# First expert matmul of a two-layer attention and mixture-of-experts kernel as three fp32r passes, split on GpSimd

## The reference

```python
# layer 0, in _moe
h = jax.nn.gelu(jnp.einsum('td,edf->etf', xf, w1) + b1[:, None, :], approximate=False)
eo = jnp.einsum('etf,efd->etd', h, w2) + b2[:, None, :]
out = jnp.einsum('etd,te->td', eo, combine)
# layer 1, in moe_ffn: eight experts and one shared one
h = jnp.einsum('nd,ehd->neh', xf, exp_w1)
h = jax.nn.silu(h)
eo = jnp.einsum('neh,edh->ned', h, exp_w2)
```

## Time and profile before

| | |
|---|---|
| time, median of 3 runs | 4743.52 us (4737.04 to 4760.26) |
| the profiled execution's own time | 4747.16 us |
| its span | 4745.7 us |
| PE busy | 4555.6 us (96%) |
| PEld busy | 2804.6 us (59%) |
| DVE busy | 3607.6 us (76%) |
| ACT busy | 2699.7 us (57%) |
| POOL busy | 696.7 us (15%) |
| mean granted clock of TensorE | 0.979 |
| HBM read | 237.40 MB |

### The profile page before, as it was taken

The page is one execution under the profiler, slowest core; times in us unless marked ns, Lnnn a source line. Parts: engine busy times, 40 slices in busy tenths (PEclk is TensorE's granted clock), DMA queues, the critical chain, the costliest instruction groups (busy, mean ns, idle before and its releaser), DMA issues.

```text
span 4745.7 us, 104925 instructions
## 1 busy us (share of the span) xinstructions
PE 4555.6 (96%) x40946; PEld 2804.6 (59%) x41312; DVE 3607.6 (76%) x9823; ACT 2699.7 (57%) x5505; POOL 696.7 (15%) x853
## 2 busy tenths in 40 slices
PE   6999999999999999999999999999999999999999
PEld 3465556666555666655565556655566556655566
DVE  5867776767777777777768888788878888788875
ACT  1566666666666667665565555555455555555554
POOL 2111212111211211121110111011110111101100
PEclk8999998999999999999999999999999999999999
DMA  2222222222222222223233323332233323332222
GB/s 68 39 52 54 50 54 59 67 58 60 48 53 54 61 67 60 58 53 75 66 99 81 80 61 89 87 89 62 76 101 81 85 61 85 103 81 79 62 70 74
DMA packets 168008, 327.22 MB, mean 69 GB/s; under 512 B 25656, under 2 KB 76624, under 8 KB 167520
## 3 DMA queue, kind: packets, MB, share of 16 engines
q1 hardware_dynamic: 167520, 320.49, 27.6%
HBM read 237.40 MB, written 4.19 MB: 51 GB/s over the span
## 4 chain that ended last, share of the span: by engine, by line
PE 79%; DVE 14%; ACT 3%; issue 2%; SPq 0%; DMA 0%; POOL 0%; DVEq 0%
PE sums L961 16%; PE b L1022 10%; PE b L1034 10%; PE b L832 9%; PE b L943 7%; PE b L933 7%; DVE chunk_max L1075 5%; PE b L856 4%; PE b L917 3%; DVE nm_s L1064 3%; DVE b L1081 3%; PE b L884 2%; ACT probs_c L1232 2%; PE b L996 2%; PE b L908 2%
## 5 line engine op out<-in xcount | busy, mean ns | idle before, releaser
L1232 ACT ACTIVATE probs_c<-b 128x512 f32<-128x512 f32 (+1 forms) x3584 | 1738.3, 572 | 1073.0 <-PE b L943 1065.0
L1081 DVE CUSTOM_DVE_ANT_0 b<-b,mcross_q 128x512 f32<-128x512 f32 (+1 forms) x2048 | 1121.1, 605 | 212.0 <-PE b L832 209.7
L1075 DVE TENSOR_REDUCE chunk_max<-b 128x1 f32<-128x512 f32 x1536 | 973.1, 683 | 139.4 <-PE b L832 134.2
L961 PE MATMUL sums<-probs_c,vc 128*32 128x256 f32 x13312 | 930.1, 395 | 0.6 <-ACT o_c L1236 0.3
L832 PE MATMUL b<-kc,qc 32*128 32x512 f32 (+1 forms) x4096 | 822.1, 412 | 17.4 <-DVE chunk_max L1075 7.1
L1034 PE MATMUL b<-w_back,hidden 128*128 128x128 f32 x4352 | 565.4, 281 | 15.5 <-DVE vc L1138 12.0
L1034 PEld LDWEIGHTS b<-w_back,hidden 128*128 128x128 f32 x4352 | 529.6, 194 | 74.6 <-ACT probs_c L1232 24.1
L832 PEld LDWEIGHTS b<-kc,qc 32*128 32x128 f32 x4096 | 425.6, 187 | 249.3 <-ACT probs_c L1232 93.2
L961 PEld LDWEIGHTS sums<-probs_c,vc 128*32 128x32 f32 x13312 | 348.0, 111 | 340.0 <-issue 166.4
L943 PE MATMUL b<-qc,kc 32*128 32x256 f32 (+1 forms) x6656 | 515.0, 336 | 17.3 <-DVE chunk_max L1077 2.2
L1022 PE MATMUL b<-xT_e,w_in 128*128 128x256 f32 x2176 | 528.5, 388 | 0.2 <-DVE chunk_max L1081 0.2
(11 more groups left out here) (159 smaller groups left out, 4497.1 us busy)
## 6 DMA issues: line engine op xcount, KB each, us to landing
w_in<-in_experts SPq DMA_DIRECT2D x272, 256.0 KB, 3.1
w_back<-in_experts SPq DMA_DIRECT2D x272, 256.0 KB, 3.3
kc<-k_hi SPq DMA_DIRECT2D x1024, 50.0 KB
ctxT<-in_ctxT SPq DMA_DIRECT2D x32, 800.5 KB, 5.2
kc<-k_lo SPq DMA_DIRECT2D x512, 50.0 KB
mask_words<-in_mcross SPq DMA_DIRECT2D x32, 800.5 KB
mask_words<-in_mcrossT SPq DMA_DIRECT2D x32, 768.0 KB
out_x<-xe SPq DMA_DIRECT2D x32, 128.0 KB, 2.0
```

What stands on the lines that cost most here:

```text
L961: last = pe.matmul(acc[HP * j:HP * j + HP, :], T["vc"][x.p][0:x.kn, v0:v0 + HP], probs_of(T, x)[0:x.kn, j, half:half + S], start=x.j == 0, ...
L1075: done = dve.tensor_reduce(best[:, x.i:x.i + 1], tile, AX, ALU.max)
L1081: done = dve.tensor_tensor_reduce(part, part, mask, 1.0, -3e38, ALU.add, ALU.max, best[:, qt:qt + 1])
L1232: act.activation(probs_of(T, x)[0:x.kn, x.j, 0:n], tile[0:x.kn, 0:n], ACT.Exp, scale=SCALE).then_inc(M["a_read"], 1)
```

## The change

The first expert product is no longer one fp32 matmul for each block, but three fp32r matmuls into the same bank: high weights by high tokens, high weights by low tokens, low weights by high tokens. (The low-by-low product is left out.) POOL makes the parts with two new steps: `EP`, one for each expert (a rounding `tensor_scalar` of 128 x 512 and a subtraction `tensor_tensor`, into `w_high` and `w_low`, two buffers of each), and `XP`, one for each round (the same for the 128 x 256 tokens). EF waits for both. `w_in` has one buffer instead of two; its next load waits for EP on POOL (`w_split`), not for EF on PE, and is issued right behind that EP in the order. EP waits for the load and for the EF that last used its pair of high and low buffers. The planner's figure for EF goes from 0.87 to 0.66, and it has figures for EP and XP. As the planner merges lists by these figures, the order of every engine is another than before.

```diff
-         "R2": 3.0, "R3": 3.0, "EBT": 1.5, "EBM": 1.0, "NS": 1.5, "ML": 8.0}
+         "R2": 3.0, "R3": 3.0, "EBT": 1.5, "EBM": 1.0, "NS": 1.5, "ML": 8.0, "EP": 2.0}
...
-POOL_US = {"LN2": 3.1, "RM2": 1.5, "RS": 0.75}
+POOL_US = {"LN2": 3.1, "RM2": 1.5, "RS": 0.75, "EP": 1.5, "XP": 0.8}
...
-        "EF": 0.87, "EBT": 0.2, "WV": 0.43, "LX": 3.0, "CL": 8.0, "KD": 10.0, "ML": 8.0, "EL": 4.0, "ST": 3.0}
+        "EF": 0.66, "EBT": 0.2, "WV": 0.43, "LX": 3.0, "CL": 8.0, "KD": 10.0, "ML": 8.0, "EL": 4.0, "ST": 3.0}
...
     def experts(self, l, p):
         count = E0 if l == 0 else E1 + 1
         out = []
+        out += self.load_expert(l, 0, 0)
         for e in range(2):
-            out += self.load_expert(l, e, 0) + self.load_expert(l, e, 1)
+            out += self.load_expert(l, e, 1)
         out += self.output(l, p)
+        out += self.split_expert(l, 0)
...
             out.append(self.put("xeT", "XT", "normed_e", l=l, role="e", p=p))
+        out.append(self.put("x_split", "XP", "xeT", l=l, p=p))
+        out += self.split_expert(l, 1)
         out.append(self.put("rt", "RT", "xeT", l=l, p=p))
...
         if l == 0:
             for e in range(0, count, 2):
+                if e:
+                    out += self.split_expert(l, e) + self.split_expert(l, e + 1)
                 piece = self.hidden(l, p, e)
                 if e:
                     piece += self.expert_out(l, p, e - 1)
                     piece += self.load_expert(l, e + 1, 1)
                 piece += self.hidden(l, p, e + 1)
-                for one in (e, e + 1):
-                    piece += self.load_expert(l, one + 2, 0) if one + 2 < count else []
                 piece += self.expert_out(l, p, e)
                 piece += self.load_expert(l, e + 2, 1) if e + 2 < count else []
                 out.append(piece)
...
         for e in range(count + 1):
             if e < count:
+                if 0 < e < count - 1:
+                    out += self.split_expert(l, e + 1)
                 out.append(self.hidden(l, p, e))
-                out += self.load_expert(l, e + 2, 0) if e + 2 < count else []
...
     def hidden(self, l, p, e):
         out = []
         for half in range(2):
-            step = self.put(("hidden", e), "EF", "xeT", l=l, p=p, i=e, c=half)
-            step.of["load"] = self.at["load", 0, e]
+            step = self.put(("hidden", e), "EF", "x_split", l=l, p=p, i=e, c=half)
+            step.of["split"] = self.at["split", e]
             out.append(step)
-        self.at["free", 0, e % EXPERT_SLOTS] = step
+        self.at["halves_free", e % EXPERT_SLOTS] = step
         return out
+
+    def split_expert(self, l, e):
+        step = self.put(("split", e), "EP", l=l, i=e)
+        step.of["load"] = self.at["load", 0, e]
+        step.of["halves_free"] = self.at.get(("halves_free", e % EXPERT_SLOTS))
+        self.at["free", 0, 0] = step
+        return [step] + (self.load_expert(l, e + 1, 0) if e + 1 < (E0 if l == 0 else E1 + 1) else [])
...
     def load_expert(self, l, e, part):
 
         step = self.put(("load", part, e), "EL", l=l, i=e, j=part)
-        step.of["free"] = self.at.get(("free", part, e % EXPERT_SLOTS))
+        step.of["free"] = self.at.get(("free", part, e % EXPERT_SLOTS if part else 0))
         return [step]
...
         elif x.kind == "EL":
-            x.slot = x.i % EXPERT_SLOTS
+            x.slot = x.i % EXPERT_SLOTS if x.j else 0
             x.c = loaded.get((x.j, x.slot), 0)
             loaded[x.j, x.slot] = x.c + 1
...
         elif x.kind == "EF":
-            load = x.of["load"]
+            slot = x.i % EXPERT_SLOTS
             if x.c == 0:
-                pe.wait_ge(M["expert_loaded", 0, load.slot], 16 * (load.c + 1))
+                pe.wait_ge(M["x_split"], nth(x.of["x_split"]))
+                pe.wait_ge(M["w_split"], nth(x.of["split"]))
             for half in range(2):
-                f = 2 * x.c + half
-                last = pe.matmul(tile[:, half * S:(half + 1) * S], T["w_in"][load.slot][:, f * P:(f + 1) * P],
-                                 T["xT_e"][:], start=True, stop=True)
+                acc, some = tile[:, half * S:(half + 1) * S], slice((2 * x.c + half) * P, (2 * x.c + half + 1) * P)
+                pe.matmul(acc, T["w_high"][slot][:, some], T["x_high"][:], start=True, stop=False)
+                pe.matmul(acc, T["w_high"][slot][:, some], T["x_low"][:], start=False, stop=False)
+                last = pe.matmul(acc, T["w_low"][slot][:, some], T["x_high"][:], start=False, stop=True)
             last.then_inc(M["a_made"], 1)
...
+        elif x.kind == "XP":
+            pool.wait_ge(M["a_read"], in_ring(x.of["xeT"]))
+            pool.tensor_scalar(T["x_high"][:], T["xT_e"][:], 1.0, 1.0, ALU.mult, ALU.mult).then_inc(M["x_rounded"], 1)
+            pool.wait_ge(M["x_rounded"], nth(x))
+            pool.tensor_tensor(T["x_low"][:], T["xT_e"][:], T["x_high"][:].bitcast(F32), ALU.subtract).then_inc(M["x_split"], 1)
+        elif x.kind == "EP":
+            load = x.of["load"]
+            high = T["w_high"][x.i % EXPERT_SLOTS][:]
+            pool.wait_ge(M["expert_loaded", 0, load.slot], 16 * (load.c + 1))
+            if "halves_free" in x.of:
+                pool.wait_ge(M["a_made"], in_ring(x.of["halves_free"]))
+            pool.tensor_scalar(high, T["w_in"][:], 1.0, 1.0, ALU.mult, ALU.mult).then_inc(M["w_rounded"], 1)
+            pool.wait_ge(M["w_rounded"], nth(x))
+            pool.tensor_tensor(T["w_low"][x.i % EXPERT_SLOTS][:], T["w_in"][:], high.bitcast(F32),
+                               ALU.subtract).then_inc(M["w_split"], 1)
...
         elif x.kind == "EL":
-            if "free" in x.of:
-                sp.wait_ge(M["d_made" if x.j else "a_made"], in_ring(x.of["free"]))
-            sp.dma_start(T["w_back" if x.j else "w_in"][x.slot][:],
+            if "free" in x.of and x.j:
+                sp.wait_ge(M["d_made"], in_ring(x.of["free"]))
+            elif "free" in x.of:
+                sp.wait_ge(M["w_split"], nth(x.of["free"]))
+            sp.dma_start(T["w_back"][x.slot][:] if x.j else T["w_in"][:],
                          t["experts"][x.l * E0 + x.i, :, x.j * FF:(x.j + 1) * FF]
                          ).then_inc(M["expert_loaded", x.j, x.slot], 16)
...
-        "hidden": pair("hidden", [P, NF, S]), "w_in": pair("w_in", [P, FF]),
+        "hidden": pair("hidden", [P, NF, S]), "w_in": sb("w_in", [P, FF]), "w_high": pair("w_high", [P, FF], F32R),
+        "w_low": pair("w_low", [P, FF], F32R),
+        "x_high": sb("x_high", [P, S], F32R), "x_low": sb("x_low", [P, S], F32R),
```

More of the change, by code:

```diff
@@ L756 @@
          "rt_exp", "rt_second", "rt_gate", "rt_done", "bias_added", "silu_done", "key_high", "rows_inverted",
-         "masks_made", "x_loaded", "ctx_loaded", "words_loaded")
+         "masks_made", "x_rounded", "x_split", "w_rounded", "w_split", "x_loaded", "ctx_loaded", "words_loaded")
 MOVES = HG * 3
```

## The result

| | median, us | ratio to before, 95% |
|---|---|---|
| before | 4744.90 (4737.04 to 4760.26, 5 runs) | |
| changed | 4784.08 (4777.00 to 4795.83, 5 runs) | 1.0091 [1.0073, 1.0108] |

The change makes the kernel 0.9% slower. I had forecast 4695 us, faster, with a range from 4640 to 4755 us. The profiled execution of the changed kernel took 4784.08 us, with a span of 4781.3.

What follows compares the result with a forecast made beforehand. The prediction took both layers as bound by PE, with DVE next. It summed 4747.2 - 105 (passes) + 51 (layer 0 waits) + 6 (DVE in layer 1) = 4699, with the median 3.6 lower: 4695 us, range 4640 to 4755.

Steps and rivals of the forecast that it cites:

- 16 x 3.2 = 51 us: Layer 0's rounds: 3.8 us of PE waits each, less 0.6 us for DVE, over 16 rounds.
- A pass at 112 ns: First expert product: fp32r passes 112 ns apart, 336 ns a block against 432, saving 105 us over 1088 blocks.
- My two neighbours: Sources of the pass price: second-product loads with matmuls, 111 ns, and SC's fp32r waves, giving 0.11 us between passes.
- The rival without overlap: First product: weights don't load under a pass, 220 ns a pass, 248 us more than now, 4992 us; chance 0.04.
- POOL near 1300 us, no bound: Splits on POOL: busy time goes from 697 to about 1300 us, 27% of the span, no bound by its sum.
- ACT at the first pair: Layer 0 round's start: ES0 can start 3.2 us after EF0, no longer hidden by EF0 and EF1; 0.5 us a round.
- ES5 and EF7 behind the key move: Layer 0: loads behind the key move on SP make ES5 wait 2.5 us and EF7 0.8 us a round.
- Layer 0 gives back what it saves: Layer 0: waits of 51 us offset the passes' saving of 49 us, so rounds keep their length.
- Layer 1: no stall, a tenth off for DVE: Layer 1: slack covers load and split; the passes save 56 us, less 6 us because DVE is at 81%.
- The clock: Layer 0: its clock, 0.97, might fall through the new gaps; named as a way to be wrong, with no term.
- The queue falls behind: Layer 0: loads behind the key move take their longest, 7.9 us a round with ACT, 4771 us; chance 0.23, all degrees.

Runs made afterwards that it cites:

- e6: The changed kernel's order with the single fp32 product of before, no splits on POOL and two w_in buffers: 4762.18 us, 1.0034 of before.
- e1: The changed kernel with two w_in staging buffers, loads two ahead, all else in the same order: 4693.37 us, 0.9888 of before.
- e2: The changed kernel, one buffer, with layer 0's key moves put behind the round's last load of w_back: 4703.07 us, 0.9933 of before.
- e4: e1 with each pass over 128 of the 256 tokens, leaving out half the product: ran once, 4682.45 us, only its trace's distances are used.
- e5: The order of before with three passes, splits on POOL and two w_in buffers: 4733.95 us, 0.9970 of before.
- e11: e8 with layer 1's key move put behind its load of w_back 7 as well: 4644.94 us, 0.9791 of before.
- e12: The changed kernel with two w_in buffers and layer 0's key moves behind the round's last load of w_back: 4690.88 us, 0.9893 of before.
- e7: e5 with one w_in buffer, each load behind the split that frees it: 4760.07 us, 1.0038 of before.
- e8: e5 with layer 0's key move put behind the load of w_back 7: 4657.21 us, 0.9824 of before.

## Why the prediction was wrong, step by step

The misses add up along the four kernels: before, e6 (new order), e1 (passes), changed (one buffer). In medians these steps are +17, -69 and +91 us; the forecast's terms for them were 0, -91 (105 less, with 8 for ACT and 6 for DVE given back) and +43 (16 rounds of 3.3 less 0.6 us). So the step that failed most is **"16 x 3.2 = 51 us"**, of which 43 us are the price of the waits behind the key move: the runs showed 91 us for one buffer, and 81 of them went with the key move's place (e2). The order, with no term, and the pass price come next.

- **A pass at 112 ns.** Mis-sized: 120 ns. A block costs 360 ns, and 1088 of them save 78 us, not 105. My two neighbours were a pass with fewer columns (111 ns) and one of a quarter of the height. The first was no clean price of a load: fp32 records start 216 ns apart at 256 columns, 123 at 144 (L1008 of the changed kernel) and 112 at 128 (L1048), all with the same load. So from 144 columns on the columns set the distance of fp32 records, and at 128 it can't be told which does. e4 shows that for a pass the columns matter little. The rival without overlap fell: passes with full-height loads follow each other in 120 ns, while the record of one load alone lasts 0.19 us, and the load of the pass shown at 1325.12 starts at 1325.00 beside the pass ahead of it. So the rule of the Trainium skill, page "TensorE: Matmul & The Clock Gate", section "What overlaps and what doesn't", which lets a weight load overlap only matmuls of another row group, does not hold for these passes. By that rule they would have been 220 ns apart, as I had worked out from the earlier trace rows.
- **POOL near 1300 us, no bound.** Right: 1270.2, 657 and 1315 ns a split; it is idle 689 us waiting for loads.
- **ACT at the first pair.** Right: ES0 starts 3.27 us behind EF0 in most rounds (3.56 before; I had 3.2). The price is 0.3 us a round, not 0.5.
- **ES5 and EF7 behind the key move.** Right in place, cause and length: 3.3 to 4.2 us together in seven of the rounds 2 to 11, against my 3.3; in the other three ES3 or EF5 wait, or both. e2 shows it by moving only those DMAs. Wrong is what I set against it: "before ... these waits don't appear". ES7 waited there already, for the same reason. So I took a kernel for bound by PE alone whose queue was at its limit in every round of layer 0.
- **Layer 0 gives back what it saves.** This failed: it gave back more, 34 us beyond the forecast. Against e1, with the same order and two buffers, layer 0 with its lead-in is 77 us longer, where I had priced the waits at 43. By length they are 3.6 us a round more idle time; but with them 2.1 us more of each round ran at the lower clock, 16 us in 15 rounds, and I had taken a wait to cost its length, less 0.6 us for DVE. Against before, by the terms: pass price, 512 x 24 ns = 12; idle 5.4 a round in place of 3.2, 33 over 15 rounds; the lead-in 6; less low clock, -16. The lead-in isn't firm: the kernels of the old order have 289.7 to 300.7 us there, those of the new one 301.0 to 304.3. Of the 5.4 us, 2.6 lie ahead of the experts' products (1.2 before, 3.8 now). The other 2.8 (0.7 to 3.5) are short waits elsewhere, and e6, without passes and with two buffers, has them all: they are the new order's own, for which I had no term. They didn't make layer 0 slower by themselves, since e6 has less low clock and a layer 0 that is 12 us shorter than before's.
- **Layer 1: no stall, a tenth off for DVE.** Half right. There is no stall of one buffer (rounds of 150.4 us in e1 and changed alike), and in the new order the passes bring 2.8 us a round there (1991.1 in e6 to 1954.7 in e1 over 13 rounds). But the new order costs 28 us in the same 13 rounds (1962.8 in before to 1991.1 in e6), and 11 in the last two (205.2 to 216.2), and gives 11 back at the turn (131.7 to 121.0). I had read the order only around the waits of layer 0, and let layer 1's stand as unchanged. How much of the miss is the order's depends on the path: with the passes it costs 7 us in the 13 rounds (1947.5 in e5 to 1954.7 in e1), while in the old order the passes bring only 15 of their 34 us there, and 13 more once the key move is out of the way (e11, 1934.8). So the queue that I had cleared for layer 1 held up the passes there too, in the old order at least; in the new one it wasn't tried.
- **The turn and the end.** One buffer adds 6 us at the turn (117.9 in e1 to 124.4) and 7 us behind the last EF0 (43.3 and 43.2 us in changed and e2, 36.1 and 36.6 in e1 and e12). No step of mine had it.
- **The clock.** Against before it didn't fall (6.0 us a round at the lower level, 8.1 before). Against e1 it did, 3.9 to 6.0, and this is the change that I had named as a risk without a term.
- **The rivals.** "The queue falls behind" is nearest with 4771, but by luck: its price, 7.1 us ahead of ES5 in every round, isn't what the runs showed (0.9 to 5.0 us ahead of a second product). None of the cases had a term for the new order or for the clock, so the chances, 0.12 on slower, were drawn too tight.

The waits of PE in layer 1 show where the new order costs. In the 13 rounds of the changed kernel the largest are:

```profile
PE b L945 <- DVE qc L1082: 10.5, 13, 0.8
PE b L1035 <- DVE chunk_max L1095: 9.3, 14, 0.7
PE b L945 <- ACT probs_s L1241: 9.2, 26, 0.5
PE b L945 <- DVE chunk_max L1095: 4.3, 26, 0.2
```

and before:

```profile
PE b L933 <- ACT probs_s L1227: 9.5, 26, 0.5
PE b L933 <- issue: 4.1, 26, 0.2
PE b L933 <- DVE chunk_max L1081: 3.2, 13, 0.3
```

The first two rows of the changed kernel, 1.5 us a round for DVE ahead of mask products (L945) and first products (L1035), have no match before. Which of the planner's new figures (0.66 for EF, the two for POOL, the lead of the split) brings them wasn't tried.

## To carry to other kernels

Before costing a saving, look for the waits that recur once in every round, however short, and follow each to what was issued ahead of it in its queue: a load that lands just in time turns the whole saving ahead of it into a wait. Here moving 12 DMAs of one queue behind the load or two that followed them was worth 30 us without the change and some 70 with it. And where an edit feeds a planner, cost its order as a part of its own, in all stages, best by a kernel that has the new order and the old work.

## What the runs showed of the hardware

- An fp32r pass of 128 rows by 128 weight columns by 256 tokens takes 120 ns with its own full load, against 432 ns for the same block in fp32: three passes are cheaper than one fp32 matmul, by 72 ns.
- A wait of PE can cost more than its length. The granted clock in e7 ahead of the wait above, in it, and in the two stretches behind it (length, busy PE, PEld, DVE, ACT, POOL, clock, DMA share, GB/s):

```profile
1304.00:1314.60 10.60, 10.44 (x96) 8.21 (x96) 5.62 (x12) 7.94 (x17) 2.90 (x3) 1.00 0.46 96
1314.60:1319.40 4.80, 0.07 (x1) 0.10 (x1) 0.85 (x3) 0.86 (x3) 0.64 (x2) 0.85 0.59 141
1319.40:1325.00 5.60, 5.60 (x38) 3.67 (x39) 2.24 (x4) 2.07 (x4) 1.24 (x1) 0.52 0.57 177
1325.00:1335.00 10.00, 9.80 (x125) 5.68 (x123) 8.18 (x19) 8.25 (x16) 3.76 (x5) 1.00 0.07 24
```

  PE worked for 10.4 of 10.6 us, was idle for 4.8, and came back at 0.52, near the lower level of 1.2 GHz: the eight records of ES7 above last 2.05 us, in before behind the short wait 1.13. A drop of 6.8 us (once 3.4) starts 2.9 to 4.3 us behind the wait's start in all of rounds 1 to 13 of e7. Without the wait (e8) nine of the 13 rounds have no drop at all, and none starts in that place: low clock 9.2 to 10.0 us a round in e7 and e5, 3.4 in e8. So removing e5's wait of 3 us made its round 5.6 us shorter. Not every drop has such a wait ahead of it: ten of the rounds 1 to 13 of before have one with no wait of PE over 0.5 us in the 10 us ahead of it. Their cause stays open.
- In the changed kernel the waits are split in two of 1.2 to 2.7 us, and in rounds 4, 7, 8 and 9 no drop follows, but in rounds 2, 10 and 11 one of 3.4 us does. The single waits of 3.4 us and more (rounds 1, 6 and 13) are all followed by one.
